# Reordering two places of a four-layer decoder kernel: first context keys before a norm, experts' norm by halves

## The reference, cut to what matters

```python
x = x + _L0_attn_ref(_layernorm(x, axis=-1), ...)
x = x + _L0_xattn_ref(8, 128, 256, L0_xattn_w, L0_xattn_u, _layernorm(x, axis=-1), ctx_2048)
x = x + _L0_ffn_ref(_layernorm(x, axis=-1), L0_ffn_router_w, L0_ffn_gate_w, L0_ffn_up_w, L0_ffn_down_w)
```

## Time and profile before

| | before |
|---|---|
| median of 3 runs (lowest to highest) | 1548.62 us (1547.56 to 1549.55) |
| the profiled execution: time / span of its trace | 1549.02 us / 1547.2 us |
| PE busy / chain that ended last, PE's share | 90% / 59% |
| DVE busy / its share of that chain | 63% / 22% |
| layer 0's cross part, from its first norm to its last residual | 54 to 108.5 us |
| experts' part: norm and routing, then chunks | 108.5 to 130.4 us, then to about 370 us |

### The profile page before, as it was taken

How to read it: one execution, slowest core, us unless ns; L and a number is a source line. 1 busy time by engine, 2 the same in 40 slices (tenths; PEclk the granted TensorE clock), 3 DMA queues, 4 the chain that set the end, 5 groups by cost and what they waited for, 6 DMA issues and landing times.

```text
span 1547.2 us, 25742 instructions
## 1 busy us (share of the span) xinstructions
PE 1391.9 (90%) x9840; PEld 878.9 (57%) x9840; DVE 980.5 (63%) x1761; ACT 732.1 (47%) x1751; POOL 455.3 (29%) x400
## 2 busy tenths in 40 slices
PE   7869999999999879999999998998996888988889
PEld 3534555555466545666666774664663545556636
DVE  6784322224678777777776787846787476685642
ACT  3452111111777456666664457458776453252230
POOL 3230000100000368776772000110925245324100
PEclk9989999999999999999999999999998798988999
DMA  8020221003100300000000100020001100000000
GB/s 253 21 89 1 67 61 31 1 0 121 43 2 3 124 7 7 8 1 8 7 7 1 76 23 0 1 82 2 2 2 71 55 1 3 2 1 3 29 0 28
DMA packets 21853, 48.11 MB, mean 31 GB/s; under 512 B 1506, under 2 KB 16995, under 8 KB 20580
## 3 DMA queue, kind: packets, MB, share of 16 engines
q1 hardware_dynamic: 21732, 46.47, 8.6%
HBM read 41.22 MB, written 5.24 MB: 30 GB/s over the span
## 4 chain that ended last, share of the span: by engine, by line
PE 59%; DVE 22%; POOL 7%; ACT 7%; issue 5%; DMA 0%; DVEq 0%; ACTq 0%; POOLq 0%
PE PS L861 43%; PE PS L1091 5%; DVE work L2572 4%; PE PS L956 3%; PE PS L1391 2%; ACT work L1696 2%; DVE small L2041 1%; PE PS L1150 1%; PE PS L873 1%; POOL work L702 1%; POOL WB L696 1%; POOL work L699 1%; POOL WB L695 1%; PE PS L1420 1%; DVE WA L2475 1%
## 5 line engine op out<-in xcount | busy, mean ns | idle before, releaser
L861 PE MATMUL PS<-XT,WB 128*128 128x512 f32 (+1 forms) x688 | 298.9, 592 | 4.8 <-DVE XT L2067 2.4
L861 PEld LDWEIGHTS PS<-XT,WB 128*128 128x128 f32 (+1 forms) x688 | 126.3, 190 | 148.2 <-issue 144.3
L1696 ACT ACTIVATE work<-PS,small 128x128 f32<-128x128 f32 x512 | 137.7, 416 | 44.0 <-DVE small L2372 44.0
L2262 DVE TENSOR_TENSOR work<-PS,work 128x512 f32<-128x512 f32 x48 | 33.1, 692 | 168.3 <-PE PS L861 168.3
L646 POOL TENSOR_SCALAR small<-small 128x4 f32<-128x4 f32 x22 | 5.1, 230 | 404.3 <-DVE small L2044 404.2
L1624 ACT ACTIVATE work<-PS 128x512 f32<-128x512 f32 x48 | 28.7, 597 | 193.5 <-PE PS L861 193.4
L2372 DVE TENSOR_REDUCE small<-PS 128x4 f32<-128x512 f32 x128 | 80.5, 685 | 40.2 <-PE PS L861 38.9
L861 PE MATMUL PS<-XT,WA 128*128 128x512 f32 (+2 forms) x224 | 97.4, 597 | 4.5 <-DVE XT L2067 2.4
L2572 DVE SCALAR_TENSOR_TENSOR work<-PS,vec,work 128x508 f32<-128x508 f32 (+2 forms) x108 | 80.2, 743 | 13.6 <-DVE work L2572 6.4
L1091 PE MATMUL PS<-WB,work 128*128 128x256 f32 x384 | 86.9, 379 | 0.5 <-DVE work L2267 0.5
L1091 PEld LDWEIGHTS PS<-WB,work 128*128 128x128 f32 x384 | 72.8, 190 | 18.3 <-issue 7.7
(11 more groups left out here) (377 smaller groups left out, 2955.9 us busy)
## 6 DMA issues: line engine op xcount, KB each, us to landing
WB<-in_l0f SPq DMA_DIRECT2D x8, 768.0 KB, 7.5
WB<-in_l1x SPq DMA_DIRECT2D x1, 6144.0 KB, 18.3
WB<-in_l0f SPq DMA_DIRECT2D x32, 96.0 KB, 7.2
WB<-in_l2f SPq DMA_DIRECT2D x1, 3072.0 KB, 9.9
WA<-in_l3a SPq DMA_DIRECT2D x1, 2624.0 KB, 9.0
WB<-in_l3f SPq DMA_DIRECT2D x1, 2064.0 KB, 8.0
WA<-in_l1f SPq DMA_DIRECT2D x1, 2056.0 KB, 12.1
C<-in_ctx SPq DMA_DIRECT2D x2, 1024.0 KB, 7.1
```

The costliest lines, as they stand in the source:

```text
L861: mm = lambda o, l, r, s, e: nc.tensor.matmul(o, l, r, start=s, stop=e)
L1696: f(wk(12288 + (u % 8) * G + h * P, P), bank(j)[:, h * P:(h + 1) * P], ACT.Exp, bias=sm(704 + (u % 8) * 4 + h, 1)).then_inc(*act_step(*([j ...
L2262: v.tensor_tensor(l0f_h(m)[:, lo:lo + G], bank(j), l0f_s(m)[:, lo:lo + G], ALU.mult).then_inc(*dve_step(j))
```

## The change

Four edits. (1) PE computes ("kc", 0) before the transposes of l0x's norm instead of behind them, and ACT sums its squares before the big exponentials instead of behind them. (2) In l0f's norm, DVE normalises half 0 behind the third residual pair instead of behind the fourth; each half's copy to XT stands directly behind its half on ACT and DVE. (3) PE computes gate and up of chunk 0, half 0, between the transposes of the two halves; only those of half 1 stay behind "rt". (4) POOL's first two copies of weights come before the `roots` of l0f's norm.

```diff
--- before.py
+++ after.py
@@ -69,16 +69,16 @@
     p = {}
     guv = [[(k, rc, g) for g in range(2) for k in ("gate", "u", "v")] for rc in range(2)]
     p["l0a"] = ln + [("h", g) for g in range(2)] + guv[0] + [("ctx", g, c) for g in range(2) for c in range(2)] + guv[1] + out
-    l = list(ln)
+    l = [("kc", 0)] + ln
     for b in range(NB + 2):
         if b < NB:
-            l += [("kc", b), ("vc", b)]
+            l += [("kc", b), ("vc", b)] if b else [("vc", b)]
         if b >= 2:
             l += [("kt", b - 2)]
     p["l0x"] = l + out
-    l = list(ln) + [("r",), ("rt",)] + [("acc", bp) for bp in range(4)]
+    l = ln[:2] + [("gate", 0, 0), ("up", 0, 0)] + ln[2:] + [("r",), ("rt",)] + [("acc", bp) for bp in range(4)]
     for m in range(CHUNKS):
-        l += [(k, m, g) for g in range(2) for k in ("gate", "up")]
+        l += [(k, m, g) for g in range(2) for k in ("gate", "up") if (m, g) != (0, 0)]
         l += [("wt",)] if m == 0 else []
         l += [("wr", q, g) for q in range(QUADS) if m == max(0, 3 * q - 1) for g in range(2)]
     p["l0f"] = l
@@ -673,13 +673,19 @@
                 pool_steps[0] += 1
                 pool.wait_ge(pool_own, pool_steps[0])
                 nc.gpsimd.tensor_tensor(sm(352 + 4 * b, 4), sm(320 + 4 * b, 4), sm(112, 4), ALU.pow).then_inc(key_roots.sem, key_roots.give())
-            roots()
-            for q in range(QUADS):
+            def side_by_side_copy(q):
+
                 pool.wait_ge(exp_in[q % QUAD_SLOTS], 80 * (q // QUAD_SLOTS + 1))
                 if q >= 2:
                     pool.wait_ge(*full(job_of["l0f", "up", 3 * q - 4, 1]))
                 nc.gpsimd.tensor_copy(quad_cols(q).rearrange("p (k e u) -> p k e u", e=4, u=32),
                                       quad(q, "gate_up").rearrange("p (e k u) -> p k e u", e=4, u=32)).then_inc(side_by_side, 1)
+
+            for q in range(2):
+                side_by_side_copy(q)
+            roots()
+            for q in range(2, QUADS):
+                side_by_side_copy(q)
             pool.wait_ge(wa_in, 32)
             for k, n in enumerate(("k", "ks")):
                 for c in range(2):
@@ -1021,18 +1027,26 @@
                 end(ins)
 
 
-            ln("l0x")
             pe.wait_ge(ctx_w_in, 16)
             for g in range(2):
                 for c in range(2):
                     pe.wait_ge(*freed(J("l0a", "ctx", g, c)))
+
+            def context(n, b):
+
+                i = ("kc", "vc").index(n)
+                o = begin("l0x", n, b)
+                for c in range(2):
+                    ins = mm(o, xt(c, b * P, (b + 1) * P, CT), ctx_w[:, (2 * i + c) * G:(2 * i + c + 1) * G], c == 0, c == 1)
+                end(ins)
+
+            context("kc", 0)
+            ln("l0x")
             for b in range(NB + 2):
+                if 1 <= b < NB:
+                    context("kc", b)
                 if b < NB:
-                    for i, n in enumerate(("kc", "vc")):
-                        o = begin("l0x", n, b)
-                        for c in range(2):
-                            ins = mm(o, xt(c, b * P, (b + 1) * P, CT), ctx_w[:, (2 * i + c) * G:(2 * i + c + 1) * G], c == 0, c == 1)
-                        end(ins)
+                    context("vc", b)
                 if b >= 2:
                     x = b - 2
                     o = begin("l0x", "kt", x)
@@ -1052,22 +1066,30 @@
                 end(ins)
 
 
-            ln("l0f")
+            def inner(m, g):
+
+                q, part = m // 3, m % 3
+                for i, n in enumerate(("gate", "up")):
+                    o = begin("l0f", n, m, g)
+                    end(from_xt(o, P, g, lambda c: quad_cols(q)[:, ((2 * i + c) * 3 + part) * P:((2 * i + c) * 3 + part + 1) * P]))
+
+            ln("l0f", (0,))
             pe.wait_ge(cst_in, 48)
             pe.wait_ge(vec_in, 16)
             need_xt("l0f", 0)
+            pe.wait_ge(side_by_side, 1)
+            inner(0, 0)
+            ln("l0f", (1,))
             need_xt("l0f", 1)
             narrow("l0f", "r", lambda c: vec("rw0", c * NE, NE))
             narrow_back("l0f", "r")
             for m in range(CHUNKS + 1):
                 if m < CHUNKS:
-                    q, part = m // 3, m % 3
-                    if part == 0:
-                        pe.wait_ge(side_by_side, q + 1)
+                    if m % 3 == 0:
+                        pe.wait_ge(side_by_side, m // 3 + 1)
                     for g in range(2):
-                        for i, n in enumerate(("gate", "up")):
-                            o = begin("l0f", n, m, g)
-                            end(from_xt(o, P, g, lambda c: quad_cols(q)[:, ((2 * i + c) * 3 + part) * P:((2 * i + c) * 3 + part + 1) * P]))
+                        if (m, g) != (0, 0):
+                            inner(m, g)
                     if m == 0:
                         o = begin("l0f", "wt").bitcast(BF16)
                         pe.wait_ge(dve_to_pe.sem, dve_to_pe.next())
@@ -1567,8 +1589,18 @@
 
             act.wait_ge(cst_in, 48)
             ln("l0x")
+            def key_sums(b):
+
+                j = J("l0x", "kc", b)
+                act.wait_ge(*full(j))
+                if b >= 2:
+                    act.wait_ge(*full(J("l0x", "kt", b - 2)))
+                for kv in range(KV):
+                    f(ctx_keys(b)[:, kv * P:(kv + 1) * P], bank(j)[:, kv * P:(kv + 1) * P], ACT.Square, accum_out=sm(288 + 4 * b + kv, 1)).then_inc(*act_step(*([key_squares] if kv == KV - 1 else [])))
+
             act.wait_ge(dve_to_act.sem, dve_to_act.next())
             f(sm(140, 4), sm(128, 4), ACT.Exp).then_inc(*act_step(act_to_dve))
+            key_sums(0)
             for c in range(2):
                 kp, ek, _, e = l0x_tiles(c)
                 act.wait_ge(dve_to_act.sem, dve_to_act.next())
@@ -1592,12 +1624,8 @@
 
             for b in range(NB + 2):
                 if b < NB:
-                    j = J("l0x", "kc", b)
-                    act.wait_ge(*full(j))
-                    if b >= 2:
-                        act.wait_ge(*full(J("l0x", "kt", b - 2)))
-                    for kv in range(KV):
-                        f(ctx_keys(b)[:, kv * P:(kv + 1) * P], bank(j)[:, kv * P:(kv + 1) * P], ACT.Square, accum_out=sm(288 + 4 * b + kv, 1)).then_inc(*act_step(*([key_squares] if kv == KV - 1 else [])))
+                    if b:
+                        key_sums(b)
                     evict_to(J("l0x", "vc", b))
                 if 1 <= b <= NB:
                     x = b - 1
@@ -1611,7 +1639,9 @@
                 if b >= 2:
                     evict_to(J("l0x", "kt", b - 2), vec("kn"))
 
-            ln("l0f")
+            for g in range(2):
+                normalise(g)
+                evac("l0f", "ln", XT, (0,), (g,))
             evac_logits("l0f", "r")
             act.wait_ge(dve_to_act.sem, dve_to_act.next())
             f(wk(4096, 256), wk(4096, 256), ACT.Exp).then_inc(*act_step(act_to_dve))
@@ -2073,13 +2103,15 @@
                     evac_half(layer, g)
                 dve.wait_ge(*dve_last())
 
-            def residual(layer):
+            def residual(layer, norm_amid=False):
                 for bp in range(4):
                     j = J(layer, "o", bp)
                     dve.wait_ge(*full(j))
                     x2 = X[:, bp * G:(bp + 1) * G]
                     v.tensor_tensor(x2, bank(j), x2, ALU.add).then_inc(*dve_step(j))
                     stats(2 * bp, 2 * bp + 1)
+                    if norm_amid and bp == 2:
+                        normalise_half(0)
                 dve.wait_ge(*dve_last())
 
             v.memset(less_magic, -MAGIC).then_inc(*dve_step())
@@ -2190,7 +2222,7 @@
                 dve.wait_ge(*dve_last())
                 v.tensor_copy(b3(y)[:, :, 0:1], b3(ctxv)[:, :, 0:1]).then_inc(*dve_step(*([dve_to_pe] if c else [])))
             dve.wait_ge(*dve_last())
-            residual("l0x")
+            residual("l0x", True)
 
 
             def topk(vals, n, k, width, v8, rl):
@@ -2231,7 +2263,10 @@
                 dve.wait_ge(*dve_last())
                 return e_
 
-            ln("l0f")
+            evac_half("l0f", 0)
+            normalise_half(1)
+            evac_half("l0f", 1)
+            dve.wait_ge(*dve_last())
             wt = wk(5376, NB * NE)
             e_ = softmax_top(J("l0f", "rt"), NE, 4, wt)
             v.tensor_tensor(wt, wt, e_, ALU.mult).then_inc(*dve_step())
```

## The result

The changed kernel takes 1553.7 us in the median of 12 runs (1550.68 to 1559.67), the kernel before 1549.09 in the same number of runs. (The two medians by themselves lie 4.6 us apart; from here on a difference in time is the ratio's.) 1549.9 was forecast, and 1552.3 was the upper end. The profiled execution took 1551.45 us (span 1549.7).

The account below looks back on a forecast made before the run. DVE's chain was taken to bound l0x, norm, router and softmax the experts' head, then dense PE. The steps summed -0.8 + 0 + 0.13 + 2.0 = +1.3 us to 1549.9; range 1546.6 to 1552.3 (8 in 10).

Parts of the forecast that it names:

- Step 1: Head of l0x: first keys fill PE's wait, transposes keep full clock, DVE starts 0.8 us sooner; ACT's squares cost 0.
- Rival (c): l0x's norm: 0.7 us of wait still lets the clock fall, transposes stay at half; +2.1, 1550.7 us; chance 0.12.
- (a): Behind "rt": the clock holds in PE's wait or comes back at once; -0.7, 1547.9 us; chance 0.15.
- (d): All clock starts at their best, nothing lost behind "rt"; -2.4, 1546.2 us; chance 0.10 with anything faster.
- (b): l0x: POOL's copies hold up DVE's reciprocal or the product behind it; full 2.9 gives +4.2, 1552.8 us; chance 0.10.
- the prediction's signs of being wrong: Wrong if PEclk stays at 1.00 behind "rt", "rt" comes over 1 us earlier, or the reciprocal is longer.
- Step 2: POOL's two copies move inside DVE's second reciprocal in l0x, ending about 98, at price 0; upper bound 2.9 us.
- Step 3: l0f's norm by halves, up to "rt": half-clock products cost what halving saves; +0.13 us, bounds -0.41 and +0.88.
- The stretch of l3f: The same scheme's 13.36 us in l3f, carried to l0f, puts "rt" at 120.16, later by 0.88 us.
- Step 4: Behind "rt": PE idles 5.4 us, the clock falls and chunk 1 starts at half; +2.0 us, from 0.6 to 3.05.

Follow-up runs that it names:

- e4: The kernel before with only POOL's first two weight copies moved ahead of the roots; ratio 0.9991 to the kernel before.
- e9: The changed kernel with banks apart for the first keys and 8 records of chunk 1, half 0, in the wait behind "rt"; ratio 1.0008 to the kernel before.
- e11: The kernel before with the l0f and POOL changes, and chunk 0, half 1, recomputed behind "rt" (gate three times, up twice); ratio 1.0028 to the kernel before.
- e1: The changed kernel with l0x's banks dealt out as before, PE's order kept as changed; ratio 1.0019 to the kernel before.
- e5: The kernel before with POOL's copies sooner and l0f's norm by halves, all chunk 0 products behind "rt"; ratio 0.9995 to the kernel before.
- e3: The kernel before with the changes of l0f and POOL alone, l0x as before; ratio 1.0018 to the kernel before.
- e6: The kernel before with only the first keys ahead of l0x's norm, in a bank of their own; ratio 0.9982 to the kernel before.
- e10: The kernel before with the l0f and POOL changes, and chunk 0, half 1, computed twice behind "rt"; ratio 1.0040 to the kernel before.
- e8: The kernel before with keys ahead (banks apart), POOL's copies sooner, and 4 gate records of chunk 1 ahead of the weights' transposes; ratio 0.9978 to the kernel before.
- e13: The same kernel as e8, run a second time for its time; ratio 0.9973 to the kernel before.

## Why the prediction was wrong

**Step 1** was right in its size for DVE (0.8 forecast, 0.73 found in the change and in every kernel with the keys ahead), and ACT's squares were hidden as said. Rival (c) has fallen: in all seven kernels with keys ahead PE still waited 0.75 us, and the sixteen transposes behind it took 2.91 us, at full clock. The step failed in the sentence that everything on the keys' side comes 1 us sooner "and nobody waits for it". I had counted instructions and not banks. Moved to the head of the plan, ("kc", 0) takes the bank of the first norm transposes, whose next user is ("kc", 2), while all later jobs keep theirs. A transposes' bank is free as soon as it is copied; a keys' bank is held until its squares are summed, POOL has the roots and ACT has scaled it (in the changed kernel block 0's products start at 53.0 and the scaling ends at 69.3). The plan's two changed lines showed that. PE lost 5.67 us, the keys' side became the end of l0x, and the cross part lost 2.4 us where 0.8 were to be won. No rival named it: (a), (c) and (d) asked only for the clock, and (b) for DVE's reciprocal. Nor did the prediction's signs of being wrong look there. None of the three came true, and the miss was at a place that none of them watches.

**Step 2** was right in its price and, in the changed kernel, wrong in its place. In e4 and the other kernels in which the copies lie in the reciprocal it takes 6.54 or 6.55 us, as without them, so rival (b) has fallen. With it falls the reading of the Trainium skill's rule (GPSIMD Engine Reference, section 1, Specifications) by which a reciprocal would be contended. In the changed kernel the copies came 5 us later than I said, at 99.46, since the keys' side was late. The reciprocal had ended at 97.4, and the copies met DVE's wait for the turning back (98.8 to 103.3).

**Step 3** was of the right kind and too small: +0.83 found, +0.13 forecast, with 0.88 as the upper bound. (By the runs it is three terms: the copies -2.1, halving +0.5, the products between the halves +2.4.) The stretch of l3f, taken as it was (120.16, +0.88), would have been the better forecast. I had shortened it by 0.75 for a milder start of the clock, but the 8 records took 5.63 us here, and 5.45 in e9, against 5.97 in l3f.

**Step 4** was right: +2.32 found, +2.0 forecast, and shown by e11 to be the clock alone. Rival (a) has fallen, and with it (d), which had nothing in step 4. The Trainium skill's rule (TensorE: Matmul & The Clock Gate, section HAM oscillation) held in the changed kernel, where PEclk fell in the 5.54 us of wait.

The range was too narrow because it held the costs only of the steps that I saw. Without the bank the sum would have been +2.4, as in e1, inside it.

## What to carry to other kernels

When a job moves in a plan that deals out buffers in turn, ask who had the buffer before, who gets it next and how long its new owner holds it; order on the engine and order of the buffers can be changed apart. Work moved ahead of a wait pays only when other work moves up into the place it leaves: here the 8 records that went ahead of "rt" cost 2.4 us there (e5 to e3; the copies' gain hides most of it in c) and left a wait that cost 2.3 behind it, while 4 records that moved up into the gap spared 1.7 us (17.95 to 16.23). Look for the small step that sits beside the critical one on a shared path (POOL's copies beside DVE's norm): moving it cost the reciprocal nothing and gave 2.1 us up to "rt", though in e4's execution the clock took 1.7 of them back.

## What the runs showed of the hardware

The same 2.47 us of wait on PE let the clock fall in some executions and not in others. Stretches of e3 and of e4 over that wait and the sixteen transposes behind it, the same instructions in both:

```profile
53.94:56.41 2.47, 0.01 (x1) 0.03 (x1) 2.32 (x8) 0.36 (x1) 0.49 (x2) 0.97 0.00 0
56.41:60.01 3.60, 3.60 (x17) 3.27 (x18) 1.68 (x5) 2.90 (x6) 0.78 (x1) 0.55 0.00 0
```

```profile
53.06:55.53 2.47, 0.00 (x1) 0.03 (x1) 2.33 (x8) 0.37 (x1) 0.50 (x2) 1.00 0.00 0
55.53:58.44 2.91, 2.80 (x17) 1.95 (x18) 1.65 (x5) 2.63 (x6) 0.77 (x1) 1.00 0.00 0
```

So the 0.7 us of step 1 are won only in executions in which the clock would have fallen, and in e4 nothing was left to win. Of the seven traces with l0x as before it fell in six. In the wait before the weights it held through 1.00 and 1.17 us (before, e6) and fell behind 1.75 and more (e4, e5, e9, e10). At layer 1's norm it held through 1.45 and 1.35 us in eleven traces and fell in three. So a wait's length alone does not say what comes behind it.

With several such places in a program, one kernel's executions differ by some us without any change. e8 and e13 are the same kernel: their profiled spans are 1535.3 and 1541.2 us, and over the last part, from 1200 us on, the granted clock is 0.92 and 0.90 in the mean.
